# First attention of a four-stage transformer block: scores as products of a row block and a column block, one row factor fewer, and the head difference taken straight from the bank of the sums

## The chip, the cores and the metric

The kernel runs on one core of one Trainium2 chip. The core has five engines that run side by side and meet through semaphores: TensorE (PE, with its weight loads as PEld), VectorE (DVE), ScalarE (ACT), GpSimd (POOL) and SyncE (SP, which only issues DMAs here). The metric is the device time of one execution in microseconds (us).

## The reference, cut to what matters

The input x has 64 batches of 128 tokens with 128 features. Four blocks follow one another, each after a layer norm and each added to x: an attention over the graph `adj` with 8 heads, a mixture of 8 experts, a graph attention with 256 features, and a feed-forward layer on half of the tokens. Only the first is touched:

```python
x_proj = jnp.einsum('bnd,hdf->bhnf', x, W)               # 8 heads of 16 features
e_src = jnp.einsum('bhnf,hf->bhn', x_proj, a_src)        # one number per token and head
e_dst = jnp.einsum('bhnf,hf->bhn', x_proj, a_dst)
e = jax.nn.leaky_relu(e_src[..., :, None] + e_dst[..., None, :], 0.2)
e = e + (beta * jnp.log(prior + EPS))[:, None, :, :]     # the prior is adj, the same for every batch
e = jnp.where(adj[None, None, :, :] > 0, e, neg_inf)
attn = jax.nn.softmax(e, axis=-1)
h = jnp.einsum('bhij,bhjf->bhif', attn, x_proj)
return h.transpose(0, 2, 1, 3).reshape(B, N, D) @ W_out.T
```

The exponential of a leaky ReLU of s_i + d_j has two forms, exp(s_i + d_j) where the sum is positive and exp(0.2 (s_i + d_j)) where it is not, and each is a product of a factor of i and a factor of j. So the kernel needs the scores only for their sign. It makes a 0/1 mask times the prior (`l_mi`), sums the values under the mask with both kinds of column factors, and puts the row factors on afterwards.

## The kernel before, in words

`build` runs `setup_phase`, `head_attention_phase` (the first attention), `experts_phase`, `combine_graph_phase` and `last_ffn_phase` one after the other. The first attention goes over 16 groups (`GROUPS`) of 4 batches (`GB`), so 32 pairs of batch and head (`HB`) in a group.

The work is laid out as a software pipeline written by hand. For every group number g, each engine runs one function (`pe_slot`, `dve_slot`, `act_slot`, `pool_slot`), which lists in a fixed order what this engine does in slot g for several groups: letter n is the layer-norm statistics of group g+3, x the projection of group g+2, y the preparation of the scores and values of group g+1, z the attention itself of group g, w the output projection of group g-1, r and l the layer norm and router logits of groups g-2 and g-3 for the next block. Slots run from -2 to 18; those from 4 to 11 are a hardware loop over pairs. Nothing but this order and the semaphores decides when something runs: an engine that waits at one line holds back everything listed after it.

What one slot holds, by the names in the trace (`l_` stands before the tiles of this phase):

- **Scores.** `pe_z_scores` makes for each of the 4 batches two halves of 4 heads, each a bank `l_sbc` of 128 x 512 sums s_i + d_j. A half is one product of 512 columns (L479, `sparts` against the selector `sel_d`) and four of 128 columns (L482, the selector `sel_s` against `sparts`). `sparts` holds the 32 rows of s and of d, each split in a bf16 part and the rest. `dve_z_compare` (L491) turns a bank into a half of the mask `l_mi`.
- **Sums.** `pe_z_sums` (L504 to L512) puts the masked sums of one batch into the one bank `l_oo`, two kinds of 17 columns for each head. `dve_z_post` (L521, L523) multiplies the two kinds by their row factors into `l_t`, two SBUF tiles, and gives the bank free (`o_read`). `dve_z_heads` (L530) subtracts them, `dve_z_rden` (L534) takes the reciprocal of the denominators, and `pool_z_post` (L541) divides.
- **Projection of group g+2.** `pe_x_transpose` (L368), `act_x_xT` (L374), `pe_x_values` (L380) make the bank `l_vs` with values and scores. `act_x_scores` (L398) copies the scores to `l_sd`, at the start of the slot after.
- **Preparation of group g+1.** `pe_y_transpose` (L407), `act_y_hi` (L412) and `dve_y_max` (L417, L418, L421) make `sparts` and the maximum of d for each head, `pe_y_maxima` (L426) spreads it to all partitions, `dve_y_small` (L434 to L439) makes the exponents `l_pk`, `act_y_exp` (L444) the factors `l_bdfg`. `pool_y_scale` (L449, L451), `pool_y_res` (L462) and `pool_y_lo` (L470), with ACT's casts between them (L457, L466), split the scaled values in three bf16 parts.
- **Output of group g-1.** `pe_w_transpose` (L551) into the bank `l_tT`, `act_w_hT` (L557), `pe_w_project` (L563), `dve_w_add` (L569).
- **Statistics of group g+3.** `dve_x_stats` (L333, L338), `act_x_rstd` (L343, L345), `dve_x_shift` (L351), `act_x_apply` (L359).

## Time and profile before

| | us |
|---|---|
| median of 3 runs (lowest, highest) | 1152.54 (1150.32, 1153.1) |
| profiled execution, its own time | 1151.04 |
| its span, from the first to the last instruction | 1149.3 |
| busy in the span: PE, PEld, DVE | 982.7, 817.2, 758.6 |
| busy in the span: ACT, POOL | 678.8, 476.0 |

The first attention takes from about 17 to 292 us of the span. Spans and starts below are counted in us from the first instruction. A busy engine is one that executes; the time from the start of one matmul to that of the next can be shorter than the duration of one, because matmuls are pipelined, so steps between starts say more than durations on PE.

### The profile page before, as it was taken

How to read it: one execution, taken by the hardware profiler on the slowest of the kernel's cores; microseconds unless marked ns; L12 is line 12 of the kernel's file. 1: busy time of each engine (PE TensorE's matmuls, PEld its weight loads, DVE VectorE, ACT ScalarE, POOL GpSimd, SP SyncE). 2: the span in 40 equal slices, each digit the busy share in tenths (PEclk: the TensorE clock that was granted, in tenths of full speed). 3: DMA queues.
4: the chain of work that ended last, by engine and by line, in shares of the span. 5: the costliest groups of instructions: out<-in, count | busy, mean ns of one | idle time of the engine just before them, and what ended most of it. 6: DMA issues, size and time to landing. Idle time of an engine off the chain costs nothing. (4 is left out here: it accounts for less than half of the span.)

```text
span 1149.3 us, 25194 instructions
## 1 busy us (share of the span) xinstructions
PE 982.7 (85%) x7932; PEld 817.2 (71%) x7980; DVE 758.6 (66%) x2314; ACT 678.8 (59%) x1670; POOL 476.0 (41%) x474
## 2 busy tenths in 40 slices
PE   1788888888899999999999925888898998559998
PEld 1577777777677799999999913565665665349997
DVE  4689999987551144455455422687887886559998
...
DMA packets 91706, 94.15 MB, mean 82 GB/s; under 512 B 16336, under 2 KB 69712, under 8 KB 90448
## 3 DMA queue, kind: packets, MB, share of 16 engines
...
q14 instruction: 51, 0.42, 0.1%
...
## 5 line engine op out<-in xcount | busy, mean ns | idle before, releaser
L1552 POOL DMA_INDIRECT g_y<-slot_rows_out,slots x128 | 128.3, 1002 | 149.3 <-SPq L1981 99.0
L1287 POOL DMA_INDIRECT slot_rows_in<-xn_all,slots x128 | 126.4, 988 | 133.1 <-DMA slot_rows_in<-xn_all,slots 83.9
L1174 ACT ACTIVATE s_hT<-s_hp,expert 128x256 f32<-128x256 f32 x284 | 113.1, 476 | 70.4 <-PE s_hp L1165 61.3
L1187 PE MATMUL s_yp<-w_experts,s_hT 128*128 x1136 | 138.4, 275 | 0.3 <-issue 0.3
L1187 PEld LDWEIGHTS s_yp<-w_experts,s_hT 128*128 128x128 f32 x1136 | 132.9, 192 | 0.7 <-issue 0.6
L1195 DVE TENSOR_TENSOR xnT_all<-s_yp,expert 128x256 f32<-128x256 f32 x71 | 30.1, 424 | 116.2 <-PE s_yp L1187 85.1
L491 DVE SCALAR_TENSOR_TENSOR l_mi<-l_sbc,mT 128x512 bf16<-128x512 f32 x128 | 86.2, 684 | 11.9 <-PE l_sbc L482 9.6
L1163 PE MATMUL s_hp<-e_xh,e_wh 128*128 128x256 f32 x284 | 85.9, 302 | 0.0
L1086 ACT ACTIVATE s_hT<-s_hp,b_shared 128x512 f32<-128x512 f32 x64 | 44.0, 687 | 65.1 <-PE s_hp L1069 54.8
L1165 PE MATMUL s_hp<-e_xh,e_wl 128*128 128x256 f32 x284 | 80.1, 282 | 0.0
L1164 PE MATMUL s_hp<-e_xl,e_wh 128*128 128x256 f32 x284 | 80.1, 282 | 0.0
L1623 PE MATMUL g_hh<-w_fc,g_r1T 128*128 128x257 f32 x256 | 67.7, 412 | 13.5 <-ACT g_h L1638 11.0
L1623 PEld LDWEIGHTS g_hh<-w_fc,g_r1T 128*128 128x128 f32 x256 | 49.5, 204 | 27.9 <-ACT g_h L1638 16.2
L541 POOL TENSOR_TENSOR l_hn<-l_heads,l_rden 128x128 f32<-128x128 f32 x64 | 25.8, 403 | 101.4 <-DVE l_rden L534 101.4
L1722 POOL TENSOR_TENSOR g_u<-g_t,g_r1T 128x1024 f32<-128x1024 f32 x16 | 42.0, 2628 | 60.2 <-DVE g_t L1717 59.7
L1077 PEld LDWEIGHTS s_yp<-w_shared,s_hT 128*128 128x128 f32 x512 | 59.4, 192 | 6.3 <-issue 6.2
L2116 POOL TENSOR_TENSOR f_wd<-f_wb,ident 128x512 f32<-128x512 f32 x16 | 21.2, 1323 | 99.7 <-ACT f_wb L2110 99.7
L1145 ACT CAST e_wh<-expert 128x512 fp32r<-128x512 f32 x71 | 44.1, 622 | 30.7 <-issue 29.6
L1069 PE MATMUL s_hp<-xnT_all,w_shared 128*128 128x512 f32 x128 | 59.8, 613 | 1.7 <-PEq L89 1.5
L1077 PE MATMUL s_yp<-w_shared,s_hT 128*128 128x128 f32 x512 | 60.0, 275 | 0.0
L2161 PE MATMUL f_yp<-w_last,f_hT 128*128 128x128 f32 x512 | 59.6, 275 | 0.0
L2161 PEld LDWEIGHTS f_yp<-w_last,f_hT 128*128 128x128 f32 x512 | 58.4, 192 | 0.1
...
## 6 DMA issues: line engine op xcount, KB each, us to landing
...
slot_rows_in<-zeros SPq DMA_DIRECT2D x9, 1024.0 KB, 12.4
...
```

Of the source, the lines that this page charges most:

```text
L491: ins = dve.scalar_tensor_tensor(mi[:, b % 2, 4 * h:4 * h + 4, :], sbc[:, h, :].rearrange("p (q i) -> p q i", q=4), 0.0, k.mT[:].unsqueeze ...
L1069: pe.matmul(hp[:, c, :], k.w1_shared[:, c * P:(c + 1) * P], k.xnT[:, bass.ds(g * GB, GB), :], start=True, stop=True).then_inc(s["sh_ps"], 1)
L1077: ins = pe.matmul(yp[p][:, b * P:(b + 1) * P], s_hT[p][:, c, b * P:(b + 1) * P], k.w2_shared[:, c, :], start=(c == 0 and b == 0), stop=(c ...
L1163: pe.matmul(out_c, wh[q % 2][:, at], xh[q % 2][:], start=True, stop=False)
L1164: pe.matmul(out_c, wh[q % 2][:, at], xl[q % 2][:], start=False, stop=False)
L1165: pe.matmul(out_c, wl[q % 2][:, at], xh[q % 2][:], start=False, stop=True).then_inc(s["h_ps"], 1)
L1174: nc.scalar.activation(hT[q % 2][:, c, :], hp[:, c, 0:TILE], ACT.Gelu, bias=wt[q][:, F + c:F + c + 1]).then_inc(s["h_ok"], 1)
L1187: ins = pe.matmul(yp[q % 2][:, h * D:(h + 1) * D], hT[q % 2][:, c, h * P:(h + 1) * P], w2, start=(c == 0 and h == 0), stop=(c == FC - 1), ...
L1287: pool.indirect_dma_start(k.rows_in, bass.IndirectOffsetOnAxis(ap=k.slots[:, c, b:b + 1], axis=0), k.xn[:, b, :], None).then_inc(scattered ...
L1552: pool.indirect_dma_start(y_slot[c][:, b, :], None, k.rows_out, bass.IndirectOffsetOnAxis(ap=k.slots[:, c, b:b + 1], axis=0))\
L1623: ins = pe.matmul(hh[:, b % 2, 0:W1C], r1T[p][:, c, b * P:(b + 1) * P], k.w_fc[:, c, 0:W1C], start=(c == 0), stop=(c == H1 - 1))
L2161: ins = pe.matmul(yp[p][:, b * P:(b + 1) * P], hT[p][:, c, b * P:(b + 1) * P], k.w2_last[:, c, :], start=(c == 0 and b == 0), stop=(c == F ...
```

## The change

It does five things, all in the first attention and its setup.

1. A half of scores becomes one product of 512 columns. For that, ACT and POOL make two new tiles per group: `col_s` (four copies of 64 rows, each kept only for one place of four, by `act_y_columns`, four activations with a scale per partition) and `row_d` (8 copies of `sparts`, each kept only for one group of four heads, by `pool_y_rows`, one operation on 128 x 1024 elements). The selectors `sel_s` and `sel_d` are gone from setup.
2. The split of s and d in a bf16 part and the rest moves ahead of the transpose: `act_x_scores` adds two small casts, the new `dve_x_parts` subtracts, and `pe_y_transpose` has a second small transpose. The projection makes 144 columns for each batch where it made 160.
3. One row factor is left out, since it cancels in the division: `l_bdfg` becomes `l_bdg` with three parts, `dve_z_post` is one multiplication (`leaked`), and `dve_z_heads` subtracts it from the other half of the bank `l_oo` itself. The bank is free after `heads_ok`.
4. On DVE `dve_z_heads` stands right behind `dve_z_post`; `dve_y_max`, `dve_y_small`, `dve_r_stats` and `dve_x_stats` stand later in the slot than before. On PE the first sums stand ahead of the maxima.
5. On ACT `act_x_scores` moves from the start of a slot to the slot before it, between `act_x_rstd` and `act_w_hT`.

```diff
...
-                dve.tensor_copy(k.w_heads[:, D:D + 16], wa[:].rearrange("p t h -> p (t h)"))
-                chain(dve.tensor_copy(k.w_heads[:, D + 16:D + 32], wa[:].rearrange("p t h -> p (t h)")))
+                chain(dve.tensor_copy(k.w_heads[:, D:D + 16], wa[:].rearrange("p t h -> p (t h)")))
...
+            wait(act, s["sd_ok"], g + 1)
+            nc.scalar.copy(sd_hi[p][:], sd[p][:].rearrange("p k b h -> p k (b h)")).then_inc(s["sd_hi"], 1)
+            wait(act, s["sd_hi"], g + 1)
+            nc.scalar.copy(sd_parts[p][:, :, 0], sd_hi[p][:]).then_inc(s["parts_hi"], 1)
+
+        def dve_x_parts(dve, g, p):
+            wait(dve, s["sd_hi"], g + 1)
+            wait(dve, s["t_ps"], g - 1)
+            dve.tensor_tensor(sd_parts[p][:, :, 1], sd[p][:].rearrange("p k b h -> p k (b h)"), sd_hi[p][:],
+                              ALU.subtract).then_inc(s["parts_lo"], 1)
...
         def pe_y_transpose(pe, g, p):
-            wait(pe, s["sd_ok"], g + 1)
+            wait(pe, s["parts_hi"], g + 1)
+            wait(pe, s["parts_lo"], g + 1)
             wait(pe, s["pk_ok"], g)
+            wait(pe, s["col_ok"], g)
             wait(pe, s["lg_ok"], g - 4)
-            pe.transpose(cc[:, 0:P], sd[p][:].rearrange("p k b h -> p (k b h)"), k.ident[:]).then_inc(s["t_ps"], 1)
+            pe.transpose(cc[:, 0:P], sd_parts[p][:].rearrange("p k s n -> p (k s n)"), k.ident[:])
+            pe.transpose(cc[0:HB, 2 * P:3 * P], sd[p][:, 1].rearrange("p b h -> p (b h)"), k.ident[:])\
+                .then_inc(s["t_ps"], 1)
 
         def act_y_hi(act, g, p):
             wait(act, s["t_ps"], g + 1)
+            wait(act, s["row_ok"], g - 1)
+            nc.scalar.copy(sparts[p][64:128, :], cc[64:128, 0:P]).then_inc(s["hi_ok"], 1)
+
+        def act_y_columns(act, g, p):
+
             wait(act, s["s_ps"], (g - 1) * 2 * GB)
-            nc.scalar.copy(sparts[p][:], cc[:, 0:P]).then_inc(s["hi_ok"], 1)
+            for q in range(4):
+                ins = nc.scalar.activation(k.col_s[p][0:64, q, :], cc[0:64, 0:P], ACT.Copy,
+                                           scale=k.in_place[0:64, q:q + 1])
+            ins.then_inc(s["col_ok"], 1)
+
...
+        def pool_y_rows(pool, g, p):
+
+            wait(pool, s["hi_ok"], g + 1)
+            wait(pool, s["s_ps"], (g - 1) * 2 * GB)
+            pool.tensor_tensor(k.row_d[p][:], sparts[p][:].unsqueeze(1).to_broadcast([P, HB // 4, P]),
+                               k.in_group[:].unsqueeze(2).to_broadcast([P, HB // 4, P]), ALU.mult)\
+                .then_inc(s["row_ok"], 1)
 
         def dve_y_max(dve, g, p):
-            wait(dve, s["hi_ok"], g + 1)
+            wait(dve, s["col_ok"], g + 1)
             wait(dve, s["dm_ps"], g)
-            dve.tensor_reduce(dmax[32:64, :], cc[32:64, 0:P], AX.X, ALU.max).then_inc(s["dg_self"], 1)
-            dve.tensor_tensor(sparts[p][64:128, :], cc[64:128, 0:P], sparts[p][64:128, :], ALU.subtract)\
-                .then_inc(s["sp_ok"], 1)
+            dve.tensor_reduce(dmax[0:HB, :], cc[0:HB, 2 * P:3 * P], AX.X, ALU.max).then_inc(s["dg_self"], 1)
             wait(dve, s["dg_self"], g + 1)
-            dve.tensor_scalar(dmdiag[32:64, :], k.diag32[32:64, :], dmax[32:64, :], None, ALU.mult)\
+            dve.tensor_scalar(dmdiag[0:HB, :], k.diag32[0:HB, :], dmax[0:HB, :], None, ALU.mult)\
                 .then_inc(s["diag_ok"], 1)
...
         def pe_z_scores(pe, g, p, b):
             if b == 0:
-                wait(pe, s["sp_ok"], g + 1)
+                wait(pe, s["col_ok"], g + 1)
+                wait(pe, s["row_ok"], g + 1)
             for h in range(2):
                 wait(pe, s["mi_ok"], g * 2 * GB + 2 * b + h - 1)
-                c = b * HEADS + 4 * h
-                pe.matmul(sbc[:, h, :].rearrange("p (q i) -> p q i", q=4), sparts[p][:], k.sel_d[:, c:c + 4, :],
-                          start=True, stop=False, skip_group_check=True)
-                for q in range(4):
-                    ins = pe.matmul(sbc[:, h, q * P:(q + 1) * P], k.sel_s[:, c + q, :], sparts[p][:],
-                                    start=False, stop=(q == 3), skip_group_check=True)
-                ins.then_inc(s["s_ps"], 1)
+                pe.matmul(sbc[:, h, :], k.row_d[p][:, 2 * b + h, :], k.col_s[p][:].rearrange("p q i -> p (q i)"),
+                          start=True, stop=True).then_inc(s["s_ps"], 1)
...
                 wait(pe, s["vb_ok"], g + 1)
-            wait(pe, s["o_read"], g * GB + b)
+            wait(pe, s["heads_ok"], g * GB + b)
...
-            dve.tensor_tensor(t1s[b % 2][:], out[:, :, 0:VW],
-                              bdfg[p][:, 2, rows].unsqueeze(2).to_broadcast([P, HEADS, VW]), ALU.mult)
-            dve.tensor_tensor(t2s[b % 2][:], out[:, :, VW:2 * VW],
-                              bdfg[p][:, 3, rows].unsqueeze(2).to_broadcast([P, HEADS, VW]), ALU.mult)\
-                .then_inc(s["o_read"], 1)
+            dve.tensor_tensor(leaked[b % 2][:], out[:, :, VW:2 * VW],
+                              bdg[p][:, 2, rows].unsqueeze(2).to_broadcast([P, HEADS, VW]), ALU.mult)\
+                .then_inc(s["leaked"], 1)
...
-            dve.tensor_tensor(heads[b % 2][:], t1s[b % 2][:], t2s[b % 2][:], ALU.subtract).then_inc(s["heads_ok"], 1)
+            wait(dve, s["leaked"], g * GB + b + 1)
+            dve.tensor_tensor(heads[b % 2][:], out[:, :, 0:VW], leaked[b % 2][:], ALU.subtract)\
+                .then_inc(s["heads_ok"], 1)
...
                 pe_y_transpose(pe, g + 1, q)
             if on["z"]:
                 pe_z_scores(pe, g, p, 1)
+            if on["z"]:
+                pe_z_sums(pe, g, p, 0)
             if on["y"]:
                 pe_y_maxima(pe, g + 1, q)
-            if on["z"]:
-                pe_z_sums(pe, g, p, 0)
...
@@ -676,56 +697,59 @@
             q = 1 - p
             if on["z"]:
                 dve_z_compare(dve, g, p, 0, 0)
+            if on["y"]:
+                dve_x_parts(dve, g + 1, q)
+            if on["z"]:
                 dve_z_compare(dve, g, p, 0, 1)
             if on["w"]:
                 dve_z_post(dve, g - 1, q, 3)
-            if on["y"]:
-                dve_y_max(dve, g + 1, q)
-            if on["w"]:
                 dve_z_heads(dve, g - 1, 3)
             if on["z"]:
                 dve_z_compare(dve, g, p, 1, 0)
             if on["w"]:
                 dve_z_rden(dve, g - 1, 3)
+            if on["z"]:
+                dve_z_compare(dve, g, p, 1, 1)
+            if on["y"]:
+                dve_y_max(dve, g + 1, q)
+            if on["z"]:
+                dve_z_post(dve, g, p, 0)
+                dve_z_heads(dve, g, 0)
             if on["y"]:
                 dve_y_small(dve, g + 1, q)
             if on["z"]:
-                dve_z_compare(dve, g, p, 1, 1)
+                dve_z_compare(dve, g, p, 2, 0)
+                dve_z_rden(dve, g, 0)
+                dve_z_compare(dve, g, p, 2, 1)
             if on["r"]:
                 dve_r_stats(dve, g - 2)
             if on["z"]:
-                dve_z_post(dve, g, p, 0)
-                dve_z_compare(dve, g, p, 2, 0)
-                dve_z_heads(dve, g, 0)
-                dve_z_compare(dve, g, p, 2, 1)
-                dve_z_rden(dve, g, 0)
+                dve_z_post(dve, g, p, 1)
...
+                dve_z_compare(dve, g, p, 3, 0)
+                dve_z_rden(dve, g, 1)
+                dve_z_compare(dve, g, p, 3, 1)
             if on["n"]:
                 dve_x_stats(dve, g + 3, q)
             if on["z"]:
-                dve_z_post(dve, g, p, 1)
-                dve_z_compare(dve, g, p, 3, 0)
-                dve_z_heads(dve, g, 1)
-                dve_z_compare(dve, g, p, 3, 1)
-                dve_z_rden(dve, g, 1)
+                dve_z_post(dve, g, p, 2)
+                dve_z_heads(dve, g, 2)
             if on["r"]:
                 dve_r_shift(dve, g - 2)
             if on["n"]:
                 dve_x_shift(dve, g + 3, q)
             if on["z"]:
-                dve_z_post(dve, g, p, 2)
+                dve_z_rden(dve, g, 2)
             if on["w"]:
                 dve_w_add(dve, g - 1, q)
-            if on["z"]:
-                dve_z_heads(dve, g, 2)
-                dve_z_rden(dve, g, 2)
             if on["l"]:
                 dve_l_logits(dve, g - 3)
...
         def act_slot(act, g, p, on):
             q = 1 - p
             if on["y"]:
-                act_x_scores(act, g + 1, q)
                 act_y_hi(act, g + 1, q)
+                act_y_columns(act, g + 1, q)
                 act_x_values(act, g + 1, q)
...
                 act_r_rstd(act, g - 2)
             if on["n"]:
                 act_x_rstd(act, g + 3, q)
+            if on["x"]:
+                act_x_scores(act, g + 2, p)
             if on["w"]:
                 act_w_hT(act, g - 1, q)
...
             if on["y"]:
+                pool_y_rows(pool, g + 1, q)
                 pool_y_scale(pool, g + 1, q)
```

The rows that follow show what an engine executes in the slot ahead of the loop (g = 3), in which every part is on. In brackets stands the semaphore that a row waits for.

On ACT before, at the end of the slot, `L343` and `L345` are `act_x_rstd`, `L557` is `act_w_hT`:

```order
L457 CAST l_vb<-l_vp 128x1088 [waits l0_pv_ps,l0_vp_ok]
L581 ACTIVATE l_lnv_r<-l_mv_r,eps_ln 128x4 [waits l0_var_r]
L583 ACTIVATE l_rstd_r<-l_lnv_r 128x4 [waits l0_lnv_r]
L343 ACTIVATE l_lnv<-l_mv,eps_ln 128x4 [waits l0_var]
L345 ACTIVATE l_rstd<-l_lnv 128x4 [waits l0_lnv_done]
L557 COPY l_hT<-l_tT 128x512 [waits l0_y_ps,l0_hT_ps]
L466 CAST l_vb<-l_vres 128x1088 [waits l0_vr_ok]
```

On ACT after, the same place; `L339` and `L341` are `act_x_rstd`, `L396` to `L402` `act_x_scores`, `L578` is `act_w_hT`:

```order
L602 ACTIVATE l_lnv_r<-l_mv_r,eps_ln 128x4 [waits l0_var_r]
L604 ACTIVATE l_rstd_r<-l_lnv_r 128x4 [waits l0_lnv_r]
L339 ACTIVATE l_lnv<-l_mv,eps_ln 128x4 [waits l0_var]
L341 ACTIVATE l_rstd<-l_lnv 128x4 [waits l0_lnv_done]
L396 COPY l_sd<-l_vs 128x2x2x8 [waits l0_t_ps,l0_parts_lo,l0_pk_ok,l0_vs_ps]
L396 COPY l_sd<-l_vs 128x2x2x8
L400 CAST l_sd_hi<-l_sd 128x64 [waits l0_sd_ok]
L402 CAST l_sd_parts<-l_sd_hi 128x2x32 [waits l0_sd_hi]
L578 COPY l_hT<-l_tT 128x512 [waits l0_y_ps,l0_hT_ps]
L491 CAST l_vb<-l_vres 128x1088 [waits l0_vr_ok]
```

Four instructions of `act_x_scores` have come between the wait for `var` and the copy `l_hT`.

On DVE before, in the second half of the slot: `L333` to `L338` are `dve_x_stats`, the four `L491` are the masks of batches 2 (second half) and 3:

```order
L491 SCALAR_TENSOR_TENSOR l_mi<-l_sbc,mT 128x512 [waits l0_s_ps]
L534 RECIPROCAL l_rden<-l_heads 128x8 [waits l0_heads_ok]
L333 BN_STATS l_st<-x_tok 128x6 [waits x_loaded3,x_loaded2]
L333 BN_STATS l_st<-x_tok 128x6 x3
L336 MEMSET l_fence 128x1 [waits l0_stats]
L338 BN_AGGR l_mv<-l_st 128x2 x4
L521 TENSOR_TENSOR l_t<-l_oo,l_bdfg 128x136 [waits l0_pv_ps,l0_heads_ok]
L523 TENSOR_TENSOR l_t<-l_oo,l_bdfg 128x136
L491 SCALAR_TENSOR_TENSOR l_mi<-l_sbc,mT 128x512 [waits l0_pv_ps,l0_s_ps]
L530 TENSOR_TENSOR l_heads<-l_t 128x136 [waits l0_o_read,l0_hn_ok]
L491 SCALAR_TENSOR_TENSOR l_mi<-l_sbc,mT 128x512 [waits l0_s_ps]
```

On DVE after, the same place: `L512` are the masks of batch 3, `L329` to `L334` are `dve_x_stats`:

```order
L542 TENSOR_TENSOR l_leaked<-l_oo,l_bdg 128x136 [waits l0_pv_ps,l0_heads_ok]
L550 TENSOR_TENSOR l_heads<-l_oo,l_leaked 128x136 [waits l0_leaked,l0_hn_ok]
L512 SCALAR_TENSOR_TENSOR l_mi<-l_sbc,mT 128x512 [waits l0_pv_ps,l0_s_ps]
L555 RECIPROCAL l_rden<-l_heads 128x8 [waits l0_heads_ok]
L512 SCALAR_TENSOR_TENSOR l_mi<-l_sbc,mT 128x512 [waits l0_s_ps]
L329 BN_STATS l_st<-x_tok 128x6 [waits x_loaded3,x_loaded2]
L329 BN_STATS l_st<-x_tok 128x6 x3
L332 MEMSET l_fence 128x1 [waits l0_stats]
L334 BN_AGGR l_mv<-l_st 128x2 x4
```

The statistics stood ahead of the masks of batch 3 and stand behind them now.

On POOL before, from the last division of group g-1 (the second of the two `L541`) on:

```order
L541 TENSOR_TENSOR l_hn<-l_heads,l_rden 128x128 [waits l0_rden_ok] x2
L449 TENSOR_TENSOR l_vp<-v_0,l_bdfg 128x32x17 [waits l0_vh_ok,l0_bdfg_ok]
L451 TENSOR_TENSOR l_vp<-v_0,l_bdfg 128x32x17
L541 TENSOR_TENSOR l_hn<-l_heads,l_rden 128x128 [waits l0_rden_ok,l0_hT_ps]
L462 TENSOR_TENSOR l_vres<-l_vp,l_vb 128x1088 [waits l0_vm_ok,l0_vh_ok]
```

And after, the same place:

```order
L562 TENSOR_TENSOR l_hn<-l_heads,l_rden 128x128 [waits l0_rden_ok] x2
L438 TENSOR_TENSOR row_d<-sparts,in_group 128x1024 [waits l0_s_ps,l0_hi_ok]
L474 TENSOR_TENSOR l_vp<-v_0,l_bdg 128x32x17 [waits l0_vh_ok,l0_bdg_ok]
L476 TENSOR_TENSOR l_vp<-v_0,l_bdg 128x32x17
L562 TENSOR_TENSOR l_hn<-l_heads,l_rden 128x128 [waits l0_rden_ok,l0_hT_ps]
L487 TENSOR_TENSOR l_vres<-l_vp,l_vb 128x1088 [waits l0_vm_ok,l0_vh_ok]
```

`L438` (`pool_y_rows`) has come in right behind the last division of the group before.

## Rows read from the trace of the kernel before

**Rows 1.** Busy time by stretch: PE, PEld, DVE, ACT, POOL, then PEclk, DMA, GB/s

```profile
55.74:237.79 182.05, 159.48 (x2284) 138.27 (x2317) 165.96 (x648) 108.06 (x288) 98.68 (x96) 0.97 0.08 31
265.60:278.50 12.90, 10.64 (x172) 9.22 (x174) 11.07 (x43) 3.88 (x10) 2.02 (x5) 1.00 0.17 63
```

**Rows 2.** Timeline of PE, one slot: start us, us, engine line op out<-in, idle before

```profile
138.19 1.33 PE L380 MATMUL l_vs<-w_heads,l_xnT 128*128 128x160 f32 x8
139.37 0.60 PE L551 MATMUL l_tT<-ident,l_hn 128*128 128x128 f32 x4
...
140.24 0.38 PE L479 MATMUL l_sbc<-sel_d,l_sparts 128*128 128x512 bf16 x1
...
140.68 0.36 PE L504 MATMUL l_oo<-l_vb,neg_mT 128*128 128x136 bf16 x3
...
141.76 1.14 PE L563 MATMUL l_yy<-w_outT,l_hT 128*128 128x128 f32 x8
142.73 0.96 PE L628 MATMUL l_cc<-w_router,l_rT 128*128 128x8 f32 x8
143.76 0.38 PE L482 MATMUL l_sbc<-l_sparts,sel_s 128*128 128x128 bf16 x4
...
148.06 0.40 PE L426 MATMUL l_cc<-l_dmdiag,ones 32*128 32x32 f32 x2 [0.70 <-DVE l_dmdiag L421]
```

**Rows 3.** Timeline of DVE, the same slot

```profile
138.48 0.83 DVE L333 BATCH_NORM_STATS2 l_st<-x_tok 128x6 f32 x4
...
139.44 0.28 DVE L338 BATCH_NORM_AGGREGATE l_mv<-l_st 128x2 f32<-128x6 f32 x3
...
140.44 0.69 DVE L491 SCALAR_TENSOR_TENSOR l_mi<-l_sbc,mT 128x512 bf16<-128x512 f32 x1 [0.33 <-PE l_sbc L482]
141.05 0.36 DVE L530 TENSOR_TENSOR l_heads<-l_t 128x136 f32<-128x136 f32 x1
...
143.66 1.31 DVE L530 TENSOR_TENSOR l_heads<-l_t 128x136 f32<-128x136 f32 x1
...
146.81 0.29 DVE L523 TENSOR_TENSOR l_t<-l_oo,l_bdfg 128x136 f32<-128x136 f32 x1
147.13 0.28 DVE L417 TENSOR_REDUCE l_dmax<-l_cc 32x1 f32<-32x128 f32 x1
...
147.77 0.23 DVE L421 TENSOR_SCALAR l_dmdiag<-diag,l_dmax 32x32 f32<-32x32 f32 x1
```

**Rows 4.** Timeline of ACT, the same slot

```profile
139.76 0.30 ACT L343 ACTIVATE l_lnv<-l_mv,eps_ln 128x4 f32<-128x4 f32 x1 [0.65 <-DVE l_mv L338]
...
140.20 0.57 ACT L557 COPY l_hT<-l_tT 128x512 f32<-128x512 f32 x1
...
143.99 0.30 ACT L398 COPY l_sd<-l_vs 128x64 f32<-128x64 f32 x2
...
149.89 0.31 ACT L444 ACTIVATE l_bdfg<-l_pk 128x128 f32<-128x128 f32 x1 [1.53 <-DVE l_pk L439]
```

**Rows 5.** Timeline of POOL, the same slot

```profile
142.56 2.25 POOL L470 TENSOR_TENSOR l_vb<-l_vres,l_vb 128x1088 bf16<-128x1088 f32 x1
...
149.25 0.41 POOL L541 TENSOR_TENSOR l_hn<-l_heads,l_rden 128x128 f32<-128x128 f32 x1 [3.56 <-DVE l_rden L534]
```

**Rows 6.** Timeline of DVE, one small operation in two slots

```profile
42.74 0.18 DVE L437 TENSOR_SCALAR l_pk<-l_pk 128x32 f32<-128x32 f32 x1
...
149.36 0.33 DVE L437 TENSOR_SCALAR l_pk<-l_pk 128x32 f32<-128x32 f32 x1
```

**Rows 7.** Busy time by stretch of 3 us (columns as in rows 1)

```profile
54.00:57.00 3.00, 1.32 (x11) 0.98 (x12) 2.84 (x10) 0.41 (x2) 0.40 (x1) 0.82 0.69 287
57.00:60.00 3.00, 3.00 (x36) 2.68 (x36) 2.53 (x10) 0.34 (x2) 1.51 (x3) 0.50 0.01 5
...
84.00:87.00 3.00, 1.57 (x28) 1.04 (x24) 2.90 (x8) 2.38 (x8) 0.87 (x2) 1.00 0.00 0
```

**Rows 8.** Timeline of ACT in setup

```profile
4.52 3.60 ACT L178 CAST sel_s<-diag_s 128x4096 bf16<-128x4096 f32 x1 [1.44 <-POOL diag_d L157]
```

More of the change, by code:

```diff
@@ L208, in chain @@
                     dve.wait_ge(dve_s, n[0])
-                dve.wait_ge(diag_made, 6)
-                dve.tensor_copy(k.sel_d[:], diag_d[:].unsqueeze(2).to_broadcast([P, HB, P]))
+                dve.wait_ge(pool_made, 7)
+                dve.tensor_reduce(k.in_group[:], k.diag32[:].rearrange("p (c q) -> p c q", q=4), AX.X, ALU.add)\
+                    .then_inc(blocks_made, 1)
+                dve.tensor_reduce(k.in_place[:], k.diag32[:].rearrange("p (c q) -> p q c", q=4), AX.X, ALU.add)\
+                    .then_inc(blocks_made, 1)
+                dve.wait_ge(blocks_made, 2)
+                for p in range(2):
+                    dve.memset(k.sparts[p][0:64], 1.0)
+                    dve.tensor_copy(k.col_s[p][64:128], k.in_place[64:128].unsqueeze(2).to_broadcast([64, 4, P]))
                 dve.wait_ge(load_adj, 32)
@@ L293, in head_attention_phase @@
         mi = sb("l0_mi", [P, 2, HEADS, P], BF16)
-        t1s = [sb(f"l0_t1{b}", [P, HEADS, VW]) for b in range(2)]
-        t2s = [sb(f"l0_t2{b}", [P, HEADS, VW]) for b in range(2)]
+        leaked = [sb(f"l0_leaked{b}", [P, HEADS, VW]) for b in range(2)]
         rdens = [sb(f"l0_rden{b}", [P, HEADS]) for b in range(2)]
@@ L899, in add_attention_buffers @@
     k.diag32, k.zeros = sb("diag32", [P, 32]), sb("zeros", [P, 2048])
-    k.sel_s, k.sel_d = sb("sel_s", [P, HB, P], BF16), sb("sel_d", [P, HB, P], BF16)
+    k.row_d = [sb(f"row_d{p}", [P, HB // 4, P], BF16) for p in range(2)]
+    k.col_s = [sb(f"col_s{p}", [P, 4, P], BF16) for p in range(2)]
+    k.sparts = [sb(f"sparts{p}", [P, P], BF16) for p in range(2)]
+    k.in_group, k.in_place = sb("in_group", [P, HB // 4]), sb("in_place", [P, 4])
     k.mT, k.neg_mT, k.neg_uT = sb("mT", [P, P], BF16), sb("neg_mT", [P, P], BF16), sb("neg_uT", [P, P])
-    k.w_heads, k.w_outT = sb("w_heads", [P, D + 32]), sb("w_outT", [P, D])
+    k.w_heads, k.w_outT = sb("w_heads", [P, D + 16]), sb("w_outT", [P, D])
     k.v17 = [sb(f"v17_{p}", [P, HB, VW]) for p in range(2)]
```

59 lines of the change are left out of this document (26 added, 33 removed).

## The prediction

> **What bounds the kernel now.** I looked first at the stretches of one slot each (busy time by stretch), to see how long a slot is and which engine fills it; then at the timelines of PE, DVE, ACT and POOL through one slot, to see who waits at which line. The stretch from the start of the `l_dmax` reduction in slot 1 to that in slot 13 is 12 slots in 182.05 us, so 15.17 us each; DVE is busy in 165.96 us of it (91%), PE in 159.48 (88%), ACT in 108.06, POOL in 98.68 [rows 1]. In the slot that I follow, DVE waits once for a score bank (0.33) before the masks [rows 3], and PE waits 0.70 for the maxima [rows 2]. So both engines are nearly full and DVE is the fuller one. Two DVE operations are longer than their size: the subtraction of SBUF tiles L530 takes 1.31 us at 143.66 and 0.36 at 141.05 [rows 3]. POOL's L470 began at 142.56 and ran for 2.25, to 144.81, and the long one ended at 144.97 [rows 5].
>
> **What gets lighter.** PE: a half of scores was 0.44 from start to start for two kinds of products that stream 512 columns each (140.24 to 140.68, [rows 2]); one is left, 0.22, and 8 halves save 1.8 us a slot. The projection took 1.18 (138.19 to 139.37, [rows 2]) for 160 columns, and by 144/160 it saves 0.1; one small transpose adds about 0.1. DVE: one product of about 0.2 less in each of 4 batches; the subtraction in the third batch no longer has two SBUF inputs and should lose its 1.0 us of waiting; L418 goes (0.3), `dve_x_parts` adds 0.2. The subtraction right behind its product has to wait for it (0.29 for a product, [rows 3]), 0.1 worse a batch. Together about 2 us less of DVE. POOL gets `row_d`: 1024 elements against 1088 in 2.25 us [rows 5], so 2.1. ACT gets four activations of 128 columns (0.31 for such a one, [rows 4]) and two small casts (0.2 each, half of the first two in [rows 4] is 0.15), 1.4 in all; it has the room.
>
> **What the order makes of it.** I walk a slot from the start of its first score product (0), all at full clock.
> - The first bank is read 0.38 after the start of its product [rows 2], so masks of batch 0 begin at 0.42. A mask takes 0.6 from start to start (140.44 to 141.05, [rows 3]). With `dve_x_parts` between them they are through at 1.8; product and subtraction of the batch before 1.8 to 2.3; masks of batch 1 with the reciprocal (0.1) between, 2.3 to 3.65. The reduction 0.28 and a hand-over [rows 3]: `l_dmdiag` is ready to start at 3.95.
> - POOL divides once the reciprocal is done (3.1), 0.4 [rows 5], and starts `row_d` at 3.5. It ends at 5.6. `l_dmdiag` is a one-input operation with an even count on SBUF, like L437, which takes 0.18 while POOL is idle and 0.33 when it begins at 149.36 inside the division of 149.25 to 149.66; it then ends at 149.69, with POOL's [rows 5, 6]. So I let `l_dmdiag` wait until 5.65: 1.5 late. POOL's start and this one hang on the same reciprocal, so they meet in every slot.
> - By the Trainium skill, SBUF — State Buffer, Who interferes with whom, a `tensor_scalar` in a mode with two ports and a GpSimd operation exclude each other for the whole instruction, and whichever starts first has the ports. That agrees with L437; no row before has `l_dmdiag` beside a POOL operation.
> - Maxima (0.40, [rows 2]) to 6.1; on DVE the product and subtraction of batch 0 fill 5.65 to 6.2, then `dve_y_small` gives the exponents at 6.7. ACT: exponential 0.31, then the copy `l_xnT`, as large as L557's 0.57 [rows 4], to 7.6. PE transposes 4 batches in 0.43 (139.37 to 140.24 less one half of scores of 0.44, [rows 2]); it has done those of group g+2 and the scores of batch 2 by 6.9 and waits for that copy until 7.6. Then router transpose to 8.05, sums 1.08 (140.68 to 141.76, [rows 2]) to 9.15, projection 1.06 to 10.2, transpose `l_tT` of the output to 10.65, scores of batch 3 from there. PE would end the next sums at 12.2 and want to project.
> - The projection needs `l_hT`, and ACT makes that now behind `act_x_scores`, which stands behind `act_x_rstd`, which waits for DVE's statistics, which stand behind the masks of batch 3. Masks from 11.1 (10.65 + 0.42) with the reciprocal: 12.4. Statistics from the first of the four to the last aggregate, 138.48 to 139.72: 1.24 [rows 3], so 13.65. `act_x_rstd` 0.44 (139.76 to 140.20) [rows 4], 14.1. Two copies in 0.30 [rows 4] and two casts with a hand-over each, 14.8. `l_hT` 0.57 [rows 4], 15.4. Before, the statistics were ahead of the masks, and L557 came right behind the transpose.
> - Projection of the output 0.97 (141.76 to 142.73, [rows 2]) and logits 0.81 (142.73 to 143.76 less the unrecorded first product of 0.22, [rows 2]): the next slot starts at 17.2. `pool_y_lo` is late too, since ACT's cast before it stands behind `l_hT`: it runs into the next slot's first 1.5 us and holds `dve_x_parts`, which has two SBUF inputs, by 0.3. **A slot is 17.5 us at full clock**, 2.3 longer than before, with 3.2 us in which PE waits before the projection.
>
> Queued behind that wait are the logits, the next scores, and so every mask; DVE's `dve_w_add` waits with them. POOL's later parts have 1 us of slack before the next sums need them.
>
> **The clock.** In the stretch 54 to 57, PE was busy 1.32 of 3.00 us, and the next 3 us ran at a granted clock of 0.50, so 1.2 GHz; from 84 to 87 it was busy 1.57 and kept 1.00, 2.4 GHz [rows 7]. Waits of 2.1 (sums to maxima), 0.7 and 3.2 us a slot are more than either. The work behind the long wait (projection and logits, 1.8 us) doubles at half clock, less what is hidden: about 1.4 a slot, so 18.9. The row that kept its clock says that not every slot need fall; I take three of four, 18.5. The Trainium skill, TensorE: Matmul & The Clock Gate, What's actually happening, says that "the default state is throttled, and activity releases the throttle"; that speaks against a change that makes PE's work lighter and its waits longer.
>
> **The sum.** Both the statistics and the output projection are on in slots 1 to 12, so 12 x (18.5 - 15.17) = +40. The last three slots have no statistics: the one of 12.90 us with 10.64 of PE and 11.07 of DVE [rows 1] loses the most, about 2.9, and the two before 0.5 and 0.8, though `l_dmdiag` still waits there: -4. In setup ACT's cast of 3.60 us [rows 8] and its like on DVE go, but the loads set the end of setup, so I take 1.4; the first slots have a longer chain to the first factors and give most of it back: -1 together (bounds -3 and +2). That is +35 to the profiled execution's own 1151.04, so **1186 us**; this execution lies 1.5 below the median of the runs, so it is within their scatter. Everything behind the first attention is untouched.
>
> **Rivals.**
> - *Full clock throughout.* 17.5 a slot: 12 x 2.33 - 5 = +23, 1174. For it: the clock held at 84 to 87 [rows 7]. Against: a wait of 3.2 us in one piece is longer than any in the slots of before.
> - *`l_dmdiag` doesn't wait for POOL.* The preparation is then 1.5 earlier at most, and a slot 16.0: 12 x 0.8 - 5 = +5, 1156; with clock falls 1170. For it: L421 never showed more than its 0.23 [rows 3], but then POOL was idle there. Against: L437 and the same kind of operands.
> - *The lighter engines and the late projection cancel*, slots of 15.5: -1, 1150.
> - *Faster: the projection isn't late.* If `l_hT` were there when PE ends the sums at 12.2, slots would be about 13.5 with DVE's and PE's lighter lists as the bound: 12 x -1.7 - 5 = -25, 1126. DVE at 91% of the slot [rows 1] speaks for it. It needs the variance 3 us earlier than I find; the point from which it decides is a slot of 15.6, 1.9 below my 17.5 at full clock, so all of POOL's hold and 0.4 us more would have to be miscounted. Against: `l_hT` can't come before masks, statistics, root and scores (1.3 + 1.24 + 0.44 + 0.7 + 0.57), which follow each other by semaphores, and PE has only 1.5 us of work beside them.
>
> **How the numbers follow.** Late projection with clock falls 0.52 (1176 to 1200); full clock 0.20 (1166 to 1182); no hold by POOL 0.10 (1152 to 1172); cancelling 0.06; faster 0.12. A difference under about 0.3% (3.5 us) can't be told from none here. The third case lies within it in a fifth of its chance, so faster 0.12, same 0.08, slower 0.80. The range leaves out the last two cases and the bottom of the third: 1160 to 1201.
>
> **What would show it.** In the trace after: slots (start of one `l_dmax` reduction to the next) of 17.5 to 19 us; a wait of about 3 us on PE at the output projection for ACT's `l_hT`, and ACT idle before `l_lnv` for DVE's `l_mv`; `l_dmdiag` at 1.5 us or more, not 0.23; a wait of 2 us on PE for it; L550 at about 0.3 everywhere; PEclk under 0.9 between 60 and 250 us. The prediction is wrong if PE meets `l_hT` ready, or if slots are under 15.6.

## The result and the profile after

The changed kernel takes 1216.02 us (median of 4 runs, 1209.76 to 1220.31) against 1152.82 of before (4 runs), a ratio of 1.0553 [1.0517, 1.0589]: slower, and by more than the range allowed. The profiled execution took 1209.76 us, its span is 1208.1, and the granted clock over the span fell from 0.948 to 0.902.

Busy time by stretch, after: the first row is nearly the stretch of rows 1, the second a single slot (columns as in rows 1).

```profile
56.16:296.00 239.84, 174.90 (x1911) 149.10 (x1932) 159.21 (x583) 122.50 (x353) 120.14 (x107) 0.76 0.06 23
112.98:134.29 21.31, 15.66 (x144) 13.18 (x146) 13.57 (x51) 10.86 (x33) 10.07 (x11) 0.70 0.07 26
```

The `l_dmax` reduction starts at 56.16 in slot 1 and at 297.90 in slot 13, so a slot is 241.74/12 = 20.15 us, against 15.17 [rows 1]. DVE was busy for 91% of a slot and is now for 66%. PE executes for 73% of it, although its list is shorter, because it does so at a mean granted clock of 0.76.

Where PE stands still, by the waits from 60 to 300 us (engine and line, then the one waited for: us in total, times, longest us):

```profile
POOL l_vb L495 <- ACT l_vb L491: 46.1, 12, 4.2
ACT l_lnv L339 <- DVE l_mv L334: 45.1, 12, 4.7
...
PE l_yy L584 <- ACT l_hT L578: 38.1, 12, 3.2
...
DVE x_tok L590 <- PE l_yy L584: 30.5, 12, 3.1
...
PE l_cc L452 <- DVE l_dmdiag L447: 18.7, 12, 2.0
```

Two waits come in each of the 12 slots: 3.2 us for `l_hT` ahead of the output projection, which was not there before, and 1.6 on average for the maxima, which was 0.70 in [rows 2]. Read from the second line: ACT makes `l_hT` late because it sat 3.8 us a slot ahead of `l_lnv`, waiting for DVE's statistics.

The timeline of PE in the slot from 154.10:

```profile
153.36 0.76 PE L533 MATMUL l_oo<-l_vb,l_mi 128*128 128x34 bf16 x24
156.02 0.63 PE L452 MATMUL l_cc<-l_dmdiag,ones 32*128 32x32 f32 x2 [1.90 <-DVE l_dmdiag L447]
156.57 1.11 PE L364 MATMUL l_tT<-ident,l_xn 128*128 128x128 f32 x4
...
161.13 1.94 PE L376 MATMUL l_vs<-w_heads,l_xnT 128*128 128x144 f32 x8
...
168.19 1.16 PE L584 MATMUL l_yy<-w_outT,l_hT 128*128 128x128 f32 x8 [3.18 <-ACT l_hT L578]
169.18 1.48 PE L649 MATMUL l_cc<-w_router,l_rT 128*128 128x8 f32 x8
```

The same slot on DVE, ACT and POOL, around the two waits:

```profile
154.42 1.54 DVE L447 TENSOR_SCALAR l_dmdiag<-diag,l_dmax 32x32 f32<-32x32 f32 x1
...
165.04 0.86 DVE L329 BATCH_NORM_STATS2 l_st<-x_tok 128x6 f32 x4
...
166.04 0.28 DVE L334 BATCH_NORM_AGGREGATE l_mv<-l_st 128x2 f32<-128x6 f32 x3
```

```profile
166.36 0.30 ACT L339 ACTIVATE l_lnv<-l_mv,eps_ln 128x4 f32<-128x4 f32 x1 [4.52 <-DVE l_mv L334]
...
167.56 0.58 ACT L578 COPY l_hT<-l_tT 128x512 f32<-128x512 f32 x1
```

```profile
153.67 0.40 POOL L562 TENSOR_TENSOR l_hn<-l_heads,l_rden 128x128 f32<-128x128 f32 x1 [4.00 <-DVE l_rden L555]
154.03 1.90 POOL L438 TENSOR_TENSOR row_d<-sparts,in_group 128x1024 bf16<-128x1024 bf16 x1
```

`row_d` ends at 155.93 and `l_dmdiag` at 155.96, 1.54 us long where it took 0.23 in [rows 3]; the maxima start at 156.02. Below, an operation of DVE is called held when it is this much longer than elsewhere and ends with an operation of POOL. The chain to the projection is statistics 165.04, `l_lnv` 166.36, `l_hT` 167.56, projection 168.19, link by link as the change wrote it.

Busy time by stretches of 2 us through the same slot; PEclk is the third column from the end:

```profile
155.00:157.00 2.00, 0.98 (x4) 0.92 (x5) 1.75 (x5) 1.15 (x3) 0.93 (x1) 0.69 0.00 0
157.00:159.00 2.00, 1.70 (x7) 0.98 (x7) 1.11 (x5) 0.87 (x2) 1.25 (x2) 0.50 0.35 131
159.00:161.00 2.00, 2.00 (x29) 1.86 (x28) 1.68 (x11) 1.18 (x2) 1.29 (x2) 0.50 0.00 0
161.00:163.00 2.00, 2.00 (x20) 2.00 (x17) 0.60 (x2) 0.81 (x3) 1.52 (x1) 0.60 0.35 131
163.00:165.00 2.00, 2.00 (x36) 1.64 (x34) 1.24 (x3) 0.00 (x0) 1.09 (x2) 1.00 0.00 0
...
169.00:171.00 2.00, 1.77 (x13) 1.72 (x13) 0.85 (x2) 1.77 (x6) 1.79 (x1) 0.61 0.00 0
171.00:173.00 2.00, 2.00 (x31) 1.65 (x31) 1.46 (x4) 0.00 (x0) 0.82 (x2) 0.50 0.00 0
```

The clock falls to 0.50 (1.2 GHz) twice in the slot: at 155.8, as the wait for the maxima ends, until 162.6, and again at 169.4, about 1 us behind the wait for `l_hT`, until past 176. In the first fall the projection L376 takes 1.94 us instead of 1.23. Read in stretches of 1 us from 56 to 300, the trace has 20 such falls in the 12 slots. One comes at the end of each of the 12 waits for `l_hT` or up to 1.5 us behind it; the other 8 come with or behind a wait for the maxima, and the remaining 4 of those waits have none. Fifteen falls last nearly 7 us and five a little over 3.

**Where the time went.** 12 slots longer by 4.98 us are +59.7. The first slots add 0.4, the slots from 13 on give back 4.4 (237.79 to the next phase's first product at 293.79 before, 297.90 to 349.52 after), and what follows, untouched, took 3.1 more. Together +58.8, from 1149.3 to 1208.1.

### The profile page after: what moved, and what is told of

Read it like the earlier page. It is cut to its first block and busy times, and to the rows that moved or that the text cites. A ratio compares the mean times of both kernels' runs of the same rounds, so it can differ in the third digit from the quotient of the medians.

```text
span 1208.1 us, 24322 instructions
## 1 busy us (share of the span) xinstructions
PE 995.5 (82%) x7452; PEld 823.3 (68%) x7484; DVE 747.6 (62%) x2238; ACT 697.1 (58%) x1765; POOL 506.0 (42%) x484
## 5 line engine op out<-in xcount | busy, mean ns | idle before, releaser
L1317 POOL DMA_INDIRECT slot_rows_in<-xn_all,slots x128 | 130.9, 1023 | 135.9 <-DMA slot_rows_in<-xn_all,slots 87.4
L512 DVE SCALAR_TENSOR_TENSOR l_mi<-l_sbc,mT 128x512 bf16<-128x512 f32 x128 | 85.8, 672 | 30.9 <-PE l_sbc L504 20.8
L1099 PE MATMUL s_hp<-xnT_all,w_shared 128*128 128x512 f32 x128 | 59.7, 612 | 1.7 <-PEq L89 1.6
L495 POOL TENSOR_TENSOR l_vb<-l_vres,l_vb 128x1088 bf16<-128x1088 f32 x16 | 36.0, 2251 | 51.7 <-ACT l_vb L491 51.7
```

The lines of the kernel that those rows point to most:

```text
L512: ins = dve.scalar_tensor_tensor(mi[:, b % 2, 4 * h:4 * h + 4, :], sbc[:, h, :].rearrange("p (q i) -> p q i", q=4), 0.0, k.mT[:].unsqueeze ...
L1099: pe.matmul(hp[:, c, :], k.w1_shared[:, c * P:(c + 1) * P], k.xnT[:, bass.ds(g * GB, GB), :], start=True, stop=True).then_inc(s["sh_ps"], 1)
L1317: pool.indirect_dma_start(k.rows_in, bass.IndirectOffsetOnAxis(ap=k.slots[:, c, b:b + 1], axis=0), k.xn[:, b, :], None).then_inc(scattered ...
```

## The experiments

"Slot" below is the mean over slots 1 to 12, between `l_dmax` reductions as above. The experiments ran on three chips, where the kernel before took 1139.30, 1131.49 and 1129.72 us. Chips differ behind the first attention (858.6 us in the profile after, 837.6 in that of `e5_wait_filled`, with the same code there), so whole times are compared by the ratio to before on the same chip and slots in us. The expectations speak of times on the chip of the result unless they name a ratio.

| run | ratio to before | slot, us |
|---|---|---|
| kernel before | 1 | 15.17 |
| changed kernel | 1.0553 [1.0517, 1.0589] | 20.15 |
| `e1_stats_early` | 1.0109 [1.0075, 1.0143] | 16.15 |
| `e2_scores_late` | 1.0473 [1.0426, 1.0519] | 19.48 |
| `e3_rows_late` | 1.0261 [1.0215, 1.0307] | 18.17 |
| `e4_all_three` | 0.9947 [0.9919, 0.9975] | 14.74 |
| `e5_wait_filled` | 1.0228 [1.0176, 1.0281] | 17.61 |
| `e6_before_stats_late` | 1.0399 [1.0330, 1.0467] | 18.66 |
| `e7_bank_alone` | 0.9807 [0.9755, 0.9858] | 13.88 |
| `e8_parts_early` | 0.9743 [0.9690, 0.9795] | 13.30 |
| `e9_fill_projection` | 1.0425 [1.0369, 1.0481] | 18.92 |
| `e10_fill_maxima` | 1.0494 [1.0462, 1.0525] | 19.93 |
| `e11_rows_first` | 0.9734 [0.9705, 0.9763] | 13.26 |

### Taking the two causes out one at a time

**e1_stats_early.** The statistics go back ahead of a batch's masks:

```diff
             if on["r"]:
                 dve_r_stats(dve, g - 2)
+            if on["n"]:
+                dve_x_stats(dve, g + 3, q)
...
                 dve_z_rden(dve, g, 1)
                 dve_z_compare(dve, g, p, 3, 1)
-            if on["n"]:
-                dve_x_stats(dve, g + 3, q)
```

> One part undone: on DVE the statistics of group g+3 stand ahead of the masks of batch 3 again (right behind the statistics for the router). My theory (the output projection waits for l_hT, which is behind act_x_rstd, which waits for DVE's statistics): the wait of about 3.2 us on PE at the output projection shrinks to under 0.5 us, slots fall from 20.1 to about 15.5 (the wait for l_dmdiag and some half clock stay), so 12 x 4.6 = 55 us less: 1150 to 1165 us. Rival (the slot is long because of POOL's new operation and the later preparation alone, the late projection only fills time that is lost anyway): the wait moves to another line and the time stays over 1195 us.

One move of an unchanged operation gives back 4.4 of the 5.5%. From 60 to 300 us PE waits for `l_hT` 2 times, 1.4 us together, where it waited 12 times and 38.1. The wait for the maxima is untouched (13 times, 21.1 us), and the slot is still 1 us above before, 0.65 above what was expected. Part of that goes with a hold that the changed kernel shows in none of slots 1 to 12, on a small DVE operation of the next block's layer norm (`l_shift_r`, 0.15 us elsewhere):

```profile
112.78 2.09 DVE L608 SCALAR_TENSOR_TENSOR l_shift_r<-l_mv_r,l_rstd_r 128x4 f32<-128x4 f32 x1
```

```profile
112.61 2.24 POOL L495 TENSOR_TENSOR l_vb<-l_vres,l_vb 128x1088 bf16<-128x1088 f32 x1 [0.45 <-ACT l_vb L491]
```

It is 1.4 us or longer in slots 4, 5, 6, 8, 10 and 12, which take 16.8 to 17.6 us; the other six take 15.0 to 15.5.

**e2_scores_late.** ACT copies `l_hT` first and makes the scores' parts after it:

```diff
-            if on["x"]:
-                act_x_scores(act, g + 2, p)
             if on["w"]:
                 act_w_hT(act, g - 1, q)
+            if on["x"]:
+                act_x_scores(act, g + 2, p)
```

> One part undone in another way: on ACT the copies of the scores stand behind l_hT and no longer ahead of it; the statistics stay late. My theory: l_hT comes about 0.75 us earlier in each of 12 slots, PE's wait before the output projection falls from 3.2 to 2.5 us, 9 us less in all at full clock: 1198 to 1208 us. Rival (the four instructions of act_x_scores are what makes the projection late, not the statistics): the wait is gone, 1160 us or less.

The wait for `l_hT` shortens by 0.8 us (28.9 in 12 times), the time of the four ACT instructions, and the slot by 0.67. By `e1_stats_early`, the greater part of the lateness is the statistics'.

**e3_rows_late.** POOL makes `row_d` behind `pool_y_scale`, so that it is not running when `l_dmdiag` wants to:

```diff
             if on["y"]:
-                pool_y_rows(pool, g + 1, q)
                 pool_y_scale(pool, g + 1, q)
+                pool_y_rows(pool, g + 1, q)
```

> On POOL the new operation row_d stands behind pool_y_scale instead of ahead of it, nothing else changed. My theory (l_dmdiag on DVE is held by the POOL operation beside it): l_dmdiag falls from 1.5 to 0.23 us, the maxima come 1.3 us earlier, PE's wait for them falls from 1.9 to about 0.6, the late projection stays: 12 to 14 x 1.3 to 2 us, 1185 to 1200 us. Rival (l_dmdiag is long for a reason of its own, or the time is made up by the late projection): l_dmdiag or the time stays as it is, over 1205 us.

All instances of one line, in the changed kernel and then in this one (ns: shortest/median/longest):

```profile
L447 DVE TENSOR_SCALAR l_dmdiag<-diag,l_dmax x16: 517/1586/1590, 29.5 to 313.2; 32x32 f32<-32x32 f32 x16
```

```profile
L447 DVE TENSOR_SCALAR l_dmdiag<-diag,l_dmax x16: 228/229/231, 29.6 to 290.1; 32x32 f32<-32x32 f32 x16
```

The same operation takes 0.229 us in every slot once `row_d` isn't beside it. So POOL's operation held it for 1.36 us. The wait for `l_hT` is as in the changed kernel (38.0, 12 times), and still the slot is 1.98 shorter, more than the 1.36. The rest goes with a higher granted clock, 0.80 on the mean of these slots against 0.76; no run separates the two.

**e4_all_three.** The three edits together.

> The three edits together: statistics early, scores behind l_hT, row_d behind pool_y_scale. My theory: no line has a wait of over 1 us on PE any more, the clock stays at 2.4 GHz, slots of about 13.5 us against 15.2 of the kernel before: 12 x -1.7 - 5, so 1120 to 1135 us, faster than both kernels. Rival (half clock comes from PE having less to do, whatever the waits): PEclk under 0.9 and slots of over 15 us, 1145 us or more.

The kernel is 0.5% faster than before, and about 2% was expected. The slot is 14.74 and not 13.5, and the granted clock is 0.89 over slots 1 to 12 where full clock was expected. Another hold stood behind the two, on `dve_x_parts`, with PE waiting for it:

```profile
124.41 1.46 DVE L407 TENSOR_TENSOR l_sd_parts<-l_sd,l_sd_hi 128x64 f32<-128x64 f32 x1
```

```profile
126.06 0.47 PE L417 MATMUL l_cc<-ident,l_sd_parts 128*128 128x128 f32 x1 [1.61 <-issue]
```

POOL's L495 ran from 123.54 to 125.79. `dve_x_parts`, with two SBUF inputs, ended at 125.87, and PE waited 1.61 us for its result; "issue" names no releaser, but the two ends say which. With shorter slots POOL's last part had moved next to it.

**e8_parts_early.** The three, and `dve_x_parts` of the next group in the slot before:

```diff
             if on["z"]:
                 dve_z_compare(dve, g, p, 0, 0)
-            if on["y"]:
-                dve_x_parts(dve, g + 1, q)
...
                 dve_z_heads(dve, g, 2)
+            if on["x"]:
+                dve_x_parts(dve, g + 2, p)
```

> The three edits together, and a fourth: dve_x_parts stands in the slot before, behind the last difference. In the run with three edits it took 1.46 us beside POOL's L495 in most slots, where 0.2 is its size, and PE waited 1.6 us for it at the transpose. My theory (a DVE operation with two SBUF inputs is held by the POOL operation beside it): PE's waits at L417 go, L407 takes 0.25 us at most, the clock holds; slots fall from 14.75 to about 13.3, 1.5 per cent less than with three edits. Rival (something else of the slot is as long): under 0.4 per cent less.

Slots of 13.30 us at a granted clock of 0.97: the change pays 2.6% once the order is mended. L407 is still held there (0.79 median, 0.25 at most was expected), but nobody waits for it. PE's largest waits are now 9.2 us in 13 times for POOL's `l_vb` and 8.4 in 10 for `l_xnT`.

**e11_rows_first.** As the last, with `pool_y_rows` ahead of the last division of the group before, where POOL was idle:

```diff
+            if on["y"]:
+                pool_y_rows(pool, g + 1, q)
             if on["w"]:
                 pool_z_post(pool, g - 1, q, 3)
             if on["y"]:
                 pool_y_scale(pool, g + 1, q)
-                pool_y_rows(pool, g + 1, q)
```

> The version with all four edits (slots of 13.28 us, ratio 0.974), with POOL's row_d ahead of the last division of a group and not behind the scaling. Theory: what is left there is POOL (PE waits for l_vb in 14 slots, 10.7 us together), and row_d placed where POOL was idle brings l_vb 1.9 us forward: slots of 12.8 to 13.1, ratio 0.966 to 0.972. Rival: row_d then runs while l_dmdiag or another DVE operation with two SBUF inputs wants to start, holds it, and gives all of it back: ratio 0.975 to 1.0, with l_dmdiag or L407 at over 1 us.

Waits of PE, from 60 to 290 us:

```profile
PE l_cc L452 <- DVE l_dmdiag L447: 8.3, 13, 1.0
...
PE l_oo L525 <- POOL l_vb L495: 1.5, 2, 0.9
```

The wait for `l_vb` went as the theory said (9.2 us in 13 times before), and one for `l_dmdiag` came in its place (0.6 in 2 before). L447 is held, as the rival said, but by 0.2 us (0.43 median, up to 1.14) of the 0.64 that PE waits each time; the run doesn't show what the rest is. The slot stays at 13.26, between the two forecasts. Its ratio and that of `e8_parts_early` can't be told apart; these two are the best versions.

### The same order on the kernel before, and the other half of the change alone

**e6_before_stats_late.** The kernel before, with only the statistics behind batch 3's masks:

```diff
-            if on["n"]:
-                dve_x_stats(dve, g + 3, q)
             if on["z"]:
                 dve_z_post(dve, g, p, 1)
...
                 dve_z_rden(dve, g, 1)
+            if on["n"]:
+                dve_x_stats(dve, g + 3, q)
```

> The kernel before with one part of the change alone: dve_x_stats stands behind the masks of batch 3. My theory: PE waits for l_hT before the output projection. Masks done at 142.0 in the slot that was shown, statistics 1.24, act_x_rstd 0.44, l_hT 0.57: ready at 144.3 where PE was ready at 141.8, so 2.5 us longer slots, with half clock behind the wait up to 4: 12 x 2.5 to 4, 2.5 to 4.2 per cent slower than before. Rival (the statistics late do harm only together with the copies of the scores ahead of l_hT): within 1 per cent of before.

This alone makes the kernel before 4.0% slower, with a wait of PE for `l_hT` of 29.8 us in 12 times and a granted clock of 0.87 in slots 1 to 12 (0.97 without the move). So most of the loss belongs to the place of the statistics, not to block products.

**e7_bank_alone.** The kernel before, with one row factor left out and the difference taken from the bank right behind its product:

```diff
-            dve.tensor_tensor(t1s[b % 2][:], out[:, :, 0:VW],
-                              bdfg[p][:, 2, rows].unsqueeze(2).to_broadcast([P, HEADS, VW]), ALU.mult)
             dve.tensor_tensor(t2s[b % 2][:], out[:, :, VW:2 * VW],
-                              bdfg[p][:, 3, rows].unsqueeze(2).to_broadcast([P, HEADS, VW]), ALU.mult)\
+                              bdfg[p][:, 2, rows].unsqueeze(2).to_broadcast([P, HEADS, VW]), ALU.mult)\
...
-            dve.tensor_tensor(heads[b % 2][:], t1s[b % 2][:], t2s[b % 2][:], ALU.subtract).then_inc(s["heads_ok"], 1)
+            dve.tensor_tensor(heads[b % 2][:], out[:, :, 0:VW], t2s[b % 2][:], ALU.subtract).then_inc(s["heads_ok"], 1)
```

> The kernel before with the other part alone: one row factor left out, the difference taken from the bank and put right behind its product; scores, setup and all other places as before. My theory: DVE loses about 1.7 us of work and of waiting for POOL in a slot, DVE bounds the slots of before (91% busy) and PE is full too at 13.6 us, so slots fall by 0.7 to 1.3: 0.7 to 1.4 per cent faster than before. Rival (the reciprocals and the hand-over of the difference cost what is saved, or PE bounds already): within 0.4 per cent.

It is 1.9% faster, where 0.7 to 1.4% was expected, so most of the 2.6% that the mended change brings is here. All 64 subtractions take 0.30 us, where L530 took 1.31 beside POOL [rows 3]. The slot loses 1.29 us. The held subtraction is 1.0 us of that; four products of about 0.2 from start to start would be 0.8 more, and some of it is given back because a subtraction now starts 0.4 us behind the product that it waits for (89.19 and 89.60). `e8_parts_early` ran on the same chip and took 1103.15 us against 1111.27 here, 0.7% less, and its slowest run (1105.75) is faster than the fastest here (1109.73). So the block products and the rest of the change, placements mended, add 0.6 to 0.7%, though the intervals of the two ratios overlap.

### What the clock took

**e5_wait_filled, e9_fill_projection, e10_fill_maxima.** In the changed kernel PE runs extra fp32 products of 128 columns, whose sums are never used, where it would stand still: 7 ahead of the maxima and 12 ahead of the output projection (e5), the 12 alone (e9), the 7 alone (e10):

```diff
+        def pe_fill(pe, g, n):
+            wait(pe, s["x_ok"], g)
+            for _ in range(n):
+                pe.matmul(yy[:, 0:P], k.neg_uT[:], k.ident[:], start=True, stop=True)
...
+            if on["y"] and on["w"]:
+                pe_fill(pe, g - 1, 7)
             if on["y"]:
                 pe_y_maxima(pe, g + 1, q)
...
+            if on["w"] and on["n"]:
+                pe_fill(pe, g - 1, 12)
             if on["w"]:
                 pe_w_project(pe, g - 1, q)
```

> The changed kernel with work for nothing put into PE's two long waits, into a bank that nothing reads then: 7 fp32 products of 128 columns ahead of the maxima (0.24 us each, 1.7 us against a wait of 1.9) and 12 ahead of the output projection (2.9 us against 3.2). No wait is shortened and PE has 4.6 us more to do in a slot; the output is the same. My theory (what I under-priced is the granted clock, 0.76 on the mean of slots 1 to 12): PEclk comes back to over 0.95 and slots fall from 20.1 to 17.5 us, so 12 x 2.6 = 31 us less than the changed kernel: 2 to 3 per cent slower than before in place of 5.5. Rival (the slot is longer than counted because of dependences that I missed, and the clock is only a sign of it): slots of 20 us or more, and no gain.

> The changed kernel with 12 extra fp32 products of 128 columns (about 2.9 us at full clock) ahead of the output projection only; their sums are never used. Filling both waits brought the slot from 20.15 to 17.7 us and the ratio from 1.055 to 1.023. If both waits cost clock, this fills the longer one (3.2 us) and gets back a part: slots of 18 to 19.2, ratio 1.03 to 1.042. If only the longer wait lets the clock fall, it gets all of it: slots of 17.7, ratio 1.023. If only the wait for the maxima does, nothing: slots of 20.1 or a little more, ratio 1.055.

> The changed kernel with 7 extra fp32 products of 128 columns (about 1.7 us at full clock) ahead of the maxima only; their sums are never used. If both waits cost clock: slots of 19 to 19.8, ratio 1.04 to 1.05. If only the longer wait lets the clock fall: slots of 20.1, ratio 1.055. If the wait for the maxima alone does: slots of 17.7, ratio 1.023.

Busy time by stretch in the three, from slot 1 on:

```profile
56.00:270.00 214.00, 195.93 (x2443) 170.19 (x2443) 162.04 (x590) 126.78 (x368) 123.05 (x111) 0.99 0.07 26
```

```profile
56.60:283.69 227.09, 189.92 (x2228) 164.47 (x2249) 161.01 (x587) 124.16 (x361) 120.56 (x109) 0.89 0.06 24
```

```profile
56.63:295.76 239.13, 192.03 (x2091) 165.83 (x2112) 160.11 (x588) 124.18 (x360) 120.15 (x109) 0.77 0.06 23
```

With both waits filled the granted clock is 0.99 and the slot 17.61 us, for more work on PE. Both engines that PE waits for are as late as in the changed kernel: PE still waits 0.4 us for `l_hT` behind the 12 products (4.8 us in 12 times) and up to 0.2 for `l_dmdiag` behind the 7. So 20.15 - 17.61 = 2.54 us a slot was clock. The other 2.44 (17.61 - 15.17) is what the waits cost at full clock, less what the lighter lists save.

One wait filled gives back less: 1.23 us for the longer, 0.22 for the shorter, 1.45 together and not 2.54. The second number has a cost of the fill in it. Where PE comes late from sums at half clock, the 7 products outlast the wait: in slots 5 to 12 the maxima begin 0.4 to 0.5 us after `l_dmdiag` has ended, in slot 1 1.26, where a hand-over takes 0.06. That is 0.37 us a slot on the mean. Even with that added the two don't reach 2.54, and the trace of `e10_fill_maxima` shows why:

```profile
162.00:164.00 2.00, 0.00 (x0) 0.00 (x0) 1.62 (x13) 1.03 (x6) 0.27 (x1) 0.85 0.00 0
164.00:166.00 2.00, 1.29 (x6) 1.29 (x7) 0.00 (x0) 2.00 (x5) 0.27 (x1) 0.50 0.00 0
...
170.00:172.00 2.00, 2.00 (x30) 1.27 (x29) 1.18 (x4) 0.69 (x3) 0.00 (x0) 0.50 0.00 0
172.00:174.00 2.00, 2.00 (x34) 1.92 (x33) 1.97 (x5) 2.00 (x9) 1.41 (x2) 0.59 0.00 0
```

```profile
164.71 2.08 PE L589 MATMUL l_yy<-w_outT,l_hT 128*128 128x128 f32 x8 [3.17 <-ACT l_hT L578]
```

From slot 2 on the clock now falls once a slot, and in slots 5 to 12 it falls within the wait and stays down for about 10 us. The projection then runs at half clock from its start (2.08 us; 1.16 in the slot of the changed kernel followed above, where the fall came behind it). In `e9_fill_projection`, with only the wait for the maxima left, the clock also falls once a slot, mostly for a little over 3 us. So the prices of the waits don't add up: the wait for the maxima alone costs 1.31 us of clock a slot (18.92 - 17.61), the one for `l_hT` alone 2.32 (19.93 - 17.61) or, less the fill's own cost, about 1.95, and both together 2.54.

## Why the prediction was right in its mechanism and wrong in its size

**Right.** The direction; the chain of masks, statistics, root, scores' parts and `l_hT`; 3.2 us of waiting ahead of the output projection (3.18); `l_dmdiag` held until `row_d` ends (1.54, predicted 1.5 or more) and about 2 us of waiting for the maxima (1.90 in the slot followed, 1.6 on the mean). The walk gave 17.5 us a slot at full clock, and `e5_wait_filled` has 17.61. L550 is 0.30 everywhere, as said. The tail gave back 4.4, predicted 4.

The Trainium skill, SBUF — State Buffer, Who interferes with whom, says that a two-port operation of DVE and one of GpSimd exclude each other for the whole instruction. `e3_rows_late` agrees: 1.586 us for `l_dmdiag` beside `row_d`, 0.229 without.

**Wrong: the clock.** The step reads "about 1.4 a slot" for the work behind the long wait, and "I take three of four, 18.5". The runs showed 2.54 us a slot instead of 1.0. Two things were mis-sized. I let only the work between the projection and the next slot (1.8 us) run at half clock, while the half clock lasted nearly 7 us in fifteen of the 20 falls. And I charged the long wait in three slots of four and the one for the maxima not at all, while the clock fell at the long wait in all 12 slots and at the other in 8 more cases. That is 12 x (20.15 - 18.5) = +20 of the 30 by which the median was off; the fixed terms are 4 (-5 predicted, -0.9 measured: +0.4, -4.4 and +3.1), and 6 that the median of the runs stands above the profiled execution. The row that "kept its clock" [rows 7] was one stretch of before, with a wait of its own length; it was too little to carry the "three of four", and the full-clock rival took its support from it.

**Wrong and small.** `row_d` took 1.90, not 2.1. `dve_x_parts` was not held in the slot followed (0.22 at 171.85), since `pool_y_lo` had ended there at 171.46. In three of its 16 instances it was (0.96, 0.46 and 1.30 us), and in `e4_all_three` PE's waits for it grew to 15.8 us in 12 times. Setup gave nothing back (slot 1 starts 0.4 later).

**The rivals.** Full clock throughout is refuted by 0.76. No hold is refuted by L447, and cancelling by the slot of 20.15. The faster case needed `l_hT` in time: `e1_stats_early` gives that, and its slot is 16.15, not the 13.5 I wrote, because the hold on `l_dmdiag` and its clock were still there and one on L608 was added; with PE no longer waiting for a held operation `e8_parts_early` has 13.30. So the rival's price was right and its condition incomplete.
